# Three waits in the loads of the opening, one swap of two loads, and another split of the last three bursts

## The reference

```
masked_w = weight * mask[None, :, :]
w_bot    = einsum('bg,got->bot', y, masked_w)
out      = x + einsum('bnt,bot->bno', x, w_bot) + bias
```

## Time and profile before

| | before |
|---|---|
| median of three runs | 602.05 us (601.76 to 602.37) |
| the profiled execution | 601.76 us |
| its span, first to last instruction | 600.0 us |
| TensorE matmuls busy | 590.8 us (98%) |
| TensorE weight loads busy | 514.3 us (86%) |
| VectorE, ScalarE, GpSimd busy | 315.3, 141.6, 38.4 us |
| moved by DMA | 148.33 MB, mean 247 GB/s |
| granted TensorE clock | 1.000 |

### The profile page before, as it was taken

One profiled execution on the slowest core, in us unless ns is written; L12 is line 12 of the kernel. 1 busy time (PEld: TensorE's weight loads), 2 busy tenths in 40 slices (PEclk: granted clock), 3 DMA queues, 4 the chain that ended last, 5 costly groups with the idle time before them and its releaser, 6 DMA issues.

```text
span 600.0 us, 14878 instructions
## 1 busy us (share of the span) xinstructions
PE 590.8 (98%) x6364; PEld 514.3 (86%) x6364; DVE 315.3 (53%) x528; ACT 141.6 (24%) x277; POOL 38.4 (6%) x34
## 2 busy tenths in 40 slices
PE   7899999999999999999999999999999999999998
PEld 5899988888888888888888888888888888889887
DVE  5565445446555555565565465465555555644343
ACT  5343222222222222222222222222222222220000
POOL 4430000000000111111110000000000000000000
DMA  9976556667766788988986776765766766767942
GB/s 326 405 283 212 185 193 234 239 214 234 235 234 218 275 280 285 348 272 302 330 298 244 242 241 227 238 219 209 276 214 210 264 222 222 251 212 244 319 147 87
DMA packets 61265, 148.33 MB, mean 247 GB/s; under 512 B 6784, under 2 KB 10240, under 8 KB 61200
## 3 DMA queue, kind: packets, MB, share of 16 engines
q1 hardware_dynamic: 40320, 113.00, 56.1%
q10 hardware_dynamic: 20880, 34.39, 15.3%
HBM read 113.81 MB, written 33.55 MB: 246 GB/s over the span
## 4 chain that ended last, share of the span: by engine, by line
PE 96%; DMA 1%; POOL 1%; SPq 1%; ACT 0%; issue 0%; DVE 0%; ACTq 0%; POOLq 0%
PE ps L461 75%; PE ps L434 20%; DMA xs<-in_mask 1%; POOL wm L202 1%; PE ps L471 1%; ACT wbot L279 0%; SPq L223 0%; SPq L229 0%; PE ps L417 0%; DVE staged L372 0%; ACTq L174 0%; POOLq L200 0%
## 5 line engine op out<-in xcount | busy, mean ns | idle before, releaser
L461 PE MATMUL ps<-wbot,xs 128*128 128x256 f32 (+1 forms) x2176 | 456.0, 368 | 1.3 <-ACT wbot L279 0.9
L461 PEld LDWEIGHTS ps<-wbot,xs 128*128 128x128 f32 x2176 | 387.2, 190 | 55.2 <-issue 3.0
L339 DVE COPY wbot<-ps 128x512 f32<-128x512 f32 (+2 forms) x272 | 164.1, 650 | 185.0 <-PE ps L461 175.1
L279 ACT ACTIVATE wbot<-ps 128x512 f32<-128x512 f32 (+2 forms) x276 | 140.3, 569 | 398.5 <-PE ps L461 198.7
L434 PEld LDWEIGHTS ps<-y_sb,wm 32*128 32x128 f32 x4096 | 122.1, 186 | 23.6 <-issue 21.5
L434 PE MATMUL ps<-y_sb,wm 32*128 32x128 f32 x4096 | 134.7, 277 | 3.7 <-POOL wm L202 2.0
L367 DVE TENSOR_TENSOR staged<-ps,staged 128x512 f32<-128x512 f32 (+1 forms) x112 | 76.5, 683 | 76.7 <-PE ps L461 76.7
L353 DVE TENSOR_TENSOR staged<-staged,bias_sb 128x512 f32<-128x512 f32 (+1 forms) x113 | 77.4, 685 | 0.0
L202 POOL TENSOR_TENSOR wm<-wm,mask_sb 128x512 f32<-128x512 f32 x16 | 21.3, 1352 | 246.2 <-DMA mask_sb<-in_mask 246.2
L367 DVE TENSOR_TENSOR staged<-ps,bias_sb 128x256 f32<-128x256 f32 (+1 forms) x24 | 12.3, 511 | 14.0 <-PE ps L461 11.5
L202 POOL TENSOR_TENSOR wm<-wm,xs 128x512 f32<-128x512 f32 x13 | 16.4, 1272 | 21.7 <-DMA xs<-in_mask 21.5
(11 more groups left out here) (4 smaller groups left out, 0.4 us busy)
## 6 DMA issues: line engine op xcount, KB each, us to landing
xs<-in_x SPq DMA_DIRECT2D x128, 512.0 KB, 4.1
out<-staged ACTq DMA_DIRECT2D x118, 256.0 KB, 4.5
staged<-in_xn SPq DMA_DIRECT2D x111, 256.0 KB, 3.7
wm<-in_w SPq DMA_DIRECT2D x12, 512.0 KB, 8.1
mask_sb<-in_mask SPq DMA_DIRECT2D x8, 512.0 KB, 8.2
out<-staged ACTq DMA_DIRECT2D x19, 128.0 KB, 4.3
wm<-in_w SPq DMA_DIRECT2D x8, 256.0 KB, 5.6
xs<-in_mask SPq DMA_DIRECT2D x4, 512.0 KB, 13.4
```

The lines of the kernel that those rows point to most:

```text
L279: eng.activation(tile_place(b, j, first, end), tile_sums(b, j, first, end), ACT.Copy).then_inc(s_ev_a, 1)
L339: eng.tensor_copy(tile_place(b, j, first, end), tile_sums(b, j, first, end)).then_inc(s_ev_v, 1)
L461: ins = eng.matmul(bank[:, h * width:(h + 1) * width], group[:, h, k, :], at, start=(k == 0), stop=(k == KT - 1))
```

## The change

SyncE waits for the mask of burst c - 3 before it issues the weights and the mask of burst c, and in the same way ahead of x of group 0, of x of group 1, and of the weights of bursts 8 and 9. ScalarE issues the mask of burst 0 ahead of y. And of the last three bursts, 125 stands alone ahead of piece 118, and 126 and 127 stand ahead of piece 119; before, it was 125 and 126, and then 127.

```diff
+    if m == FIRST_OF_LAST - 2:
+        return (BURSTS - 3,)
     if m == FIRST_OF_LAST - 1:
-        return (BURSTS - 1,)
+        return (BURSTS - 2, BURSTS - 1)
     return () if n % 2 or m >= FIRST_OF_LAST else (n + CS - 1, n + CS)
...
             for c in range(HALF):
+                if c >= 3:
+                    eng.wait_ge(s_mask[c - 3], 16)
                 load_w(0, c, 1)
+            eng.wait_ge(s_mask[HALF - 3], 16)
             load_x(0)
+            eng.wait_ge(s_mask[HALF - 2], 16)
             load_x(1)
+            eng.wait_ge(s_mask[HALF - 1], 16)
             load_w(0, 8, 2)
...
+            eng.dma_start(first_mask[:, 0, :], mask[0, :, 0, :]).then_inc(s_mask[0], 16)
             eng.dma_start(y_sb[:, 0, :], yblk[0]).then_inc(s_y, 16)
-            eng.dma_start(first_mask[:, 0, :], mask[0, :, 0, :]).then_inc(s_mask[0], 16)
             eng.wait_ge(s_blank, 1)
```

## The result

| | before | after |
|---|---|---|
| median | 602.21 us (6 runs, 601.74 to 602.99) | 605.50 us (6 runs, 605.12 to 605.87) |
| ratio, 95% interval | | 1.0054 (1.0043 to 1.0065) |
| span of the profiled execution | 600.0 us | 603.3 us |
| TensorE matmuls busy | 590.8 us | 592.3 us |
| granted TensorE clock | 1.000 | 0.997 |

The forecast was 601.0 us, with a range of 600.2 to 602.4 and a chance of 0.08 for slower. The measured time is outside.

A forecast was written before the change was run, and what follows sets the result against it. TensorE's pieces and bursts hold 95% of the chain, so only its standstills, the opening and the stop ahead of burst 127, can be won. Gains 0.25 + 0 + 0.8 = 1.05 us, from median 602.05 to 601.0 us; range 600.2 to 602.4.

The forecast's parts named there:

- the opening: Start until piece 0 begins at 19.49 us: one of two places where TensorE stands still that the change touches.
- the stop ahead of burst 127: TensorE's one stop after the opening, at 536.5 us; the new split was to remove it.
- the stop at burst 6: TensorE idle 1.49 us from 14.85 us, read as out of instructions; waits shrink it to 0 to 0.45.
- Part 1: SyncE's waits in the opening: landings unchanged, smaller backlog brings instructions sooner; gain 0.25 us, bounds 0 to 0.75.
- 2.2 < 2.6: SyncE's load queue: 2.2 us outside a fresh load's transfer, covered by 2.6 us of transfer still under way.
- rival C: Load queue runs dry under the waits; mask of bursts 8 and 9 2 to 3 us late, 603.75 us; chance 0.13.
- Part 1, the backlog: SyncE's queue falls from 2.9 to at most 1.6 MB, so the instruction transfer starts by 12.7, not 13.78 us.
- Part 2: Mask 0 ahead of y on ScalarE: worth 0, between -0.1 and +0.1 us.
- Part 3: Split of the last bursts: burst 125 to piece 119 takes 6.78 us, not 7.56; gain 0.78, bounds 0.5 to 0.85.
- what x can catch up: In rival C, x's loads recover part of mask 7's 3.7 us delay, leaving 2 to 3 us.

The follow-up runs named there:

- the last kernel above: Kernel before with nine 32-column matmuls replacing the two large ones at TensorE's start, plus the new split of the last three bursts: 601.23 us, -0.84 us.
- small_start: Kernel before with the two large matmuls at TensorE's start replaced by nine of 32 columns: -0.06 us, ratio 0.9997.
- swap_only: Kernel before with only mask 0 issued ahead of y: +0.10 us, ratio 1.0001.

## Why the prediction was wrong, step by step

**Where the kernel is bound.** Right: the opening and the stop ahead of burst 127; beside them only 0.28 us moved. Right too that the stop at burst 6 is one of instructions, and not of masks or products as the chain has it, and that nearly all of it is hidden behind the mask of bursts 8 and 9: in the last kernel above it was gone, and piece 2 began when it had before.

**Part 1, the step that failed:** "2.2 < 2.6: the queue doesn't run dry". The 2.2 us "outside the transfer" were taken from the very first load, with nothing under way beside it. The weights of burst 5 took 4.3 us, 3.7 of them outside their own 0.66 us, and 3.7 is more than the 2.6 us that two bursts cover. With three bursts the queue runs dry, with four (3.9 us of cover) the kernel is no slower: the loss ends where 3.7 puts it and not where 2.2 did. The loop of rival C was the right mechanism, with 5.4 us in the place of 4.3 to 7.1: it said the mask of 8 and 9 2 to 3 us late, and it was 4.0. That it said mask 7 at 18.4, where it landed at 18.14, is luck in part: it had mask 4 at 11.9 and 6.5 us from there to mask 7; mask 4 came on time at 10.71, and the step took 7.43, some 1.4 of it for the instruction packet, which the loop does not contain. It had a chance of 0.13 because the first load spoke against it. The same trace also held mask 1, issued at 1.63 with 1 MB asked for ahead of it and landed 4.5 us later, and the 5.4 us of mask 2; they were put down to queueing, without asking how much queueing there can be so early. Nor did the prediction ask what becomes of a wait for a mask when one engine of the 16 is late.

**Part 1, the backlog.** "An instruction transfer then starts by 12.7": it started at 13.83, as before (13.79), with half the backlog. In the other kernels with two to three and a half bursts it came at 11.5 to 12.6, in those with more at 12.6 to 15.0, while TensorE's pace differed too; whether a shorter queue brings it sooner stays open. In the changed kernel it did not, which is what the packet-wise turns of the Trainium skill (DMA: Bandwidth & Descriptors, queues, rings and completion order) would give. The bias, on ScalarE's queue, speaks the other way: its first packet came 3.5 us after its issue before, 1.2 us after it in the changed kernel, and it took 4.6 us in place of 7.7. At most 0.25 us hung on this step.

**Part 2.** Right: +0.10 measured, 0 forecast.

**Part 3.** Right in mechanism and size: 0.78 worked out, 0.79 in the trace of the changed kernel, 0.84 between the medians of its own kernel.

**Sum.** -0.25 + 0 - 0.8 was forecast; it was +3.9 in the trace for part 1, +0.1 (nothing that can be told) for part 2 and -0.8 for part 3. The price of C, 2.5, was low because "what x can catch up" was nothing: x of group 1 was itself held back to 16.9 and landed at 22.8.

## What to carry to other kernels

What a cap leaves under way must cover the time from issue to landing, less its own transfer, of a load with the engines busy (3.7 us here), not that of the first load on idle ones (2.2): here three bursts (1.5 MB) cost 3.4 us, four cost nothing that can be told, and no depth gained anything. A wait for a whole load is a wait for the slowest of its 16 parts: what puts one engine back, an instruction packet here, then stops them all. A chain in which the same kind of DMA follows itself rung by rung was here the sign that the cap, and not the bandwidth, set the pace. When a stop is followed by no semaphore, look for what the engine itself must fetch before building a gain on it, and see which other wait ends right behind it.

## What the runs showed of the hardware that was not expected

A busy share of 0.88 of the DMA engines went with 201 GB/s, where 1.05 went with 397: six packets of 113 lasted 0.31 to 1.79 us, while the median stayed at 0.084.

The Trainium skill (DMA: Bandwidth & Descriptors, anatomy of one DMA, which is about GpSimd's path) gives a fixed cost of about 2 us beside the bytes. The first load's 2.2 us agree with it; the 3.7 us of the weights of burst 5, under load, do not, and it is these that decide how many must be under way.

Around an instruction packet the loads of q1 land late, since one of their 16 parts does: 0.7 us in the kernel before (x of group 0 comes 2.0 us after mask 7, x of group 1 1.3 after it), 1.5 us in small_start and 1.3 in swap_only, all with a full queue, and 2.5 us in the changed kernel (the weights of burst 6, at 16.2, come 3.2 us after mask 5 instead of 0.7). The difference between 2.5 and 1.3 to 1.5 is about what its engine was behind before the packet began. Why single packets last up to 1.79 us while little is queued stays open.
